# One of three counts per search step moved from VectorE to ScalarE, which sums signs, in the expert routing of a fused transformer kernel

## The reference

```python
def balanced_assignment(scores):          # scores: [8192 tokens, 8 experts]
    T, E = scores.shape
    C = T // E
    taken = jnp.zeros((T,), dtype=bool)
    parts = []
    for e in range(E):
        s = jnp.where(taken, -jnp.inf, scores[:, e])
        _, idx = jax.lax.top_k(s, C)
        parts.append(idx)
        taken = taken.at[idx].set(True)
    return jnp.concatenate(parts)
```

## Time and profile before

| | |
|---|---|
| median of 3 runs | 2756.76 us (2747.97 to 2757.8) |
| the profiled execution | 2750.51 us, its span 2748.7 us |
| share of the span: PE, DVE, ACT, POOL | 75%, 72%, 56%, 44% |
| mean granted TensorE clock | 0.89 of full speed |
| routing, first score to last expert | 1084 to 1347 us |
| of it the 112 search steps with what lies between them | 1132.1 to 1338.9 us |
| scatter of the tokens behind it | 1347.5 to some 1440 us |

### The profile page before, as it was taken

One profiled execution on the slowest core, in us unless ns is written; L12 is line 12 of the kernel. 1 busy time (PEld: TensorE's weight loads), 2 busy tenths in 40 slices (PEclk: granted clock), 3 DMA queues, 4 the chain that ended last, 5 costly groups with the idle time before them and its releaser, 6 DMA issues. The chain is left out here.

```text
span 2748.7 us, 73587 instructions
## 1 busy us (share of the span) xinstructions
PE 2061.8 (75%) x26748; PEld 1195.5 (43%) x26748; DVE 1992.3 (72%) x5289; ACT 1552.3 (56%) x2872; POOL 1218.4 (44%) x1067
## 2 busy tenths in 40 slices
PE   5988989888988896411009928888888888888587
PEld 3776767676767675400004402232222322322354
DVE  4676767676777666688407817898888988987698
ACT  5665656565655563100004416787777777877587
POOL 5666666666667562000263357632432343230122
PEclk9999999999999998555559968999999999999799
DMA  4333333333333331000022232221112212220001
GB/s 115 75 79 72 71 77 74 75 80 72 79 76 75 71 73 25 1 0 0 19 64 76 81 70 49 51 41 27 25 32 34 33 26 31 35 32 2 13 23 35
DMA packets 103680, 136.73 MB, mean 50 GB/s; under 512 B 23781, under 2 KB 78981, under 8 KB 103046
## 3 DMA queue, kind: packets, MB, share of 16 engines
q1 hardware_dynamic: 99206, 123.34, 20.7%
q0 software_dynamic: 4096, 8.40, 1.1%
HBM read 26.52 MB, written 12.58 MB: 14 GB/s over the span
## 5 line engine op out<-in xcount | busy, mean ns | idle before, releaser
L1788 DVE TENSOR_REDUCE d_nmax_<-d_s_ 128x2 bf16<-128x1024 f32 x512 | 614.9, 1222 | 128.6 <-PE d_s_ L1950 126.9
L1699 ACT ACTIVATE d_pT_<-d_t_ 128x512 f32<-128x512 f32 x1024 | 558.2, 601 | 170.8 <-PE d_t_ L1962 163.3
L268 POOL TENSOR_TENSOR a_other<-a_other,a_rope 128x512 f32<-128x512 f32 x256 | 323.2, 1284 | 358.0 <-DMA a_other<-a_raw 357.2
L1975 PE MATMUL d_o_<-d_pT_,d_v_ 128*32 128x256 f32 x4096 | 326.3, 403 | 0.2 <-ACT d_pT_ L1699 0.2
L1962 PE MATMUL d_t_<-d_qs_,d_ks_ 49*128 49x512 bf16 x1024 | 207.7, 402 | 86.8 <-ACT d_pT_ L1699 41.6
L336 ACT ACTIVATE a_pT<-a_t 64x384 f32<-64x384 f32 x512 | 248.3, 485 | 19.2 <-PE a_t L588 7.5
L476 DVE RECIPROCAL a_rden<-a_o 128x512 f32<-128x512 f32 x64 | 214.7, 3355 | 49.5 <-PE a_o L601 49.4
L299 ACT COPY a_v<-a_proj 128x512 f32<-128x512 f32 x128 | 74.9, 585 | 278.8 <-PE a_proj L499 278.8
L460 DVE TENSOR_REDUCE a_nmax<-a_s 128x4 bf16<-128x384 f32 x256 | 130.7, 552 | 134.7 <-PE a_s L565 134.3
L1950 PE MATMUL d_s_<-d_ks_,d_qs_ 48*128 48x512 bf16 x1024 | 206.9, 400 | 17.5 <-DVE d_nmax_ L1788 12.1
L1155 ACT ACTIVATE c_hT_<-c_in_,c_beta_,c_gamma_ 128x512 f32<-128x512 f32 x16 | 12.4, 777 | 328.0 <-PE c_in_ L1275 328.0
(11 more groups left out here) (260 smaller groups left out, 4641.6 us busy)
## 6 DMA issues: line engine op xcount, KB each, us to landing
a_other<-a_raw SPq DMA_DIRECT2D x512, 128.0 KB, 2.3
d_qs_<-d_part_ SPq DMA_DIRECT2D x192, 64.0 KB
d_ks_<-d_part_ SPq DMA_DIRECT2D x192, 64.0 KB
a_xpre<-x SPq DMA_DIRECT2D x16, 256.0 KB, 3.8
a_xres<-x SPq DMA_DIRECT2D x16, 256.0 KB, 3.5
c_xs_<-sorted_x SPq DMA_DIRECT2D x16, 256.0 KB, 2.7
c_w_<-e_w SPq DMA_DIRECT2D x16, 256.0 KB, 3.3
sorted_x<-c_xs_ SPq DMA_DIRECT2D x16, 256.0 KB, 2.0
```

The lines of the kernel that those rows point to most:

```text
L268: nc.gpsimd.tensor_tensor(other[s % 2][:, side, :], other[s % 2][:, side, :], rope[:, 1, :], ALU.mult).then_inc(rope2_done, 1)
L1699: nc.scalar.activation(pT[kt][pair][:, a, :], t_bank(j, turn)[:], ACT.Exp).then_inc(t_read, 1)
L1788: nc.vector.reduce_max(out, s_bank(unit, e)[:], AX_X, negate=True).then_inc(s_read, 1)
L1975: ins = nc.tensor.matmul(o_ps[HC * i:HC * (i + 1), cols], v[e.k][:, kt, g * GH + i, :], pT[kt][i // 2][:, i % 2, cols], start=(kt, half) = ...
```

## The change

In a search step VectorE counts for the first two thresholds only. For the third, ScalarE takes the sign of (threshold - value) over the same 64 values with an accumulator output, in one ACTIVATE. The threshold is shifted by 0.5, so that no value equals it. The sum of signs is 64 - 2 x (count), and so the count is 32 - 0.5 x (sum of signs). TensorE puts this together in column 2 of `tot`: a matmul of ones with `halves` (which holds 32) that is issued ahead of time, and one of a matrix of -0.5 with `signs`. The sums thus come from three matmuls in place of one. `tot` is now two PSUM tiles used in turn. Some constants are set at the start of the routing.

```diff
-        count = sb("count", [128, TIES], BF16)
+        count = sb("count", [128, TIES - 1], BF16)
+        signs = sb("signs", [128, 1], BF16)
+        junk_s = sb("junk_s", [128, TILES])
+        minus_half = sb("minus_half", [128, 128], BF16)
+        halves = sb("halves", [128, 1], BF16)
...
-        tot = ps("tot", [128, 512])
+        tot = [ps(f"tot{k}", [128, 512]) for k in range(2)]
...
+            def signed(values, e, n, link):
+
+                act.wait_ge(chain, PER * e + DONE + link)
+                with nc.allow_low_precision(reason="whole numbers up to 64"):
+                    nc.scalar.activation(junk_s[:], values, ACT.Sign, bias=tries[:, TIES - 1:TIES], scale=-1.0,
+                                         accum_out=signs[:]).then_inc(signs_ready, 1)
+                act.wait_ge(signs_ready, 2 * DIGITS * e + n + 1)
+
+            with act.Fori(0, E - 1) as e:
+                for d in range(DIGITS):
+                    signed(a1[:], e, d, 1 + 3 * d if d else 2)
+                for d in range(DIGITS):
+                    signed(b1[:], e, DIGITS + d, 3 * (DIGITS + 1 + d) if d else 3 * DIGITS + 4)
...
             with pe.Fori(0, E - 1) as e:
                 for n in range(CNT):
-                    pe.wait_ge(cnt_ready, CNT * e + n + 1)
-                    nc.tensor.matmul(tot[:, 0:TIES], ones[:], count[:], start=True, stop=True).then_inc(tot_ready, 1)
+                    tot_n = tot[n % 2]
+                    if n % (DIGITS + 1) < DIGITS:
+                        nc.tensor.matmul(tot_n[:, 2:3], ones[:], halves[:], start=True, stop=True,
+                                         skip_group_check=True)
+                        pe.wait_ge(cnt_ready, CNT * e + n + 1)
+                        nc.tensor.matmul(tot_n[:, 0:2], ones[:], count[:], start=False, stop=True,
+                                         skip_group_check=True)
+                        pe.wait_ge(signs_ready, 2 * DIGITS * e + n - n // (DIGITS + 1) + 1)
+                        nc.tensor.matmul(tot_n[:, 2:3], minus_half[:], signs[:], start=False, stop=True,
+                                         skip_group_check=True).then_inc(tot_ready, 1)
...
+            nc.vector.memset(halves[:], TILES / 2.0)
...
+            nc.vector.memset(minus_half[:], -0.5).then_inc(set_ready, 1)
...
                     for d in reversed(range(DIGITS)):
-                        for k in range(TIES):
+                        for k in range(TIES - 1):
                             ins = nc.vector.tensor_scalar(junk[:, k, :], values, tries[:, k:k + 1], None, ALU.is_ge,
                                                           ALU.add, accum_out=count[:, k:k + 1])
```

More of the change, by code:

```diff
@@ L749, in routing @@
         cnt_ready = sem("cnt_ready")
+        signs_ready = sem("signs_ready")
+        set_ready = sem("set_ready")
         tot_ready = sem("tot_ready")
@@ L757, in routing @@
         CNT = 2 * DIGITS + 2
+        PER = 6 * DIGITS + 14
+        DONE = 5
         GROUPS = TILES // G4
@@ L833, in _ @@
             scores(GROUPS - 1, 1)
+            pe.wait_ge(set_ready, 1)
             def ranks(flags, n):
@@ L842, in _ @@
                 for n in range(CNT):
-                    pe.wait_ge(cnt_ready, CNT * e + n + 1)
-                    nc.tensor.matmul(tot[:, 0:TIES], ones[:], count[:], start=True, stop=True).then_inc(tot_ready, 1)
+                    tot_n = tot[n % 2]
[8 more added lines that the diff above has]
+                                         skip_group_check=True).then_inc(tot_ready, 1)
+                    else:
+                        pe.wait_ge(cnt_ready, CNT * e + n + 1)
+                        nc.tensor.matmul(tot_n[:, 0:2], ones[:], count[:], start=True, stop=True,
+                                         skip_group_check=True).then_inc(tot_ready, 1)
                 ranks(tied, 2 * e + 1)
@@ L864, in _ @@
             nc.vector.memset(count[:], 0.0)
+            nc.vector.memset(halves[:], TILES / 2.0)
             for d in range(DIGITS):
                 for k in range(TIES):
-                    nc.vector.memset(steps[:, d, k:k + 1], float((k + 1) * 4 ** d))
+                    nc.vector.memset(steps[:, d, k:k + 1], (k + 1) * 4.0 ** d - (0.5 if k == TIES - 1 else 0.0))
             for k in range(TIES):
-                nc.vector.memset(first[:, k:k + 1], float((k + 1) * 4 ** (DIGITS - 1) + 1))
+                nc.vector.memset(first[:, k:k + 1],
+                                 (k + 1) * 4.0 ** (DIGITS - 1) + (0.5 if k == TIES - 1 else 1.0))
+            nc.vector.memset(minus_half[:], -0.5).then_inc(set_ready, 1)
             def kept(m, k):
@@ L900, in _ @@
             link(nc.vector.tensor_scalar(lo1[:], half_j[:], 1.0, None, ALU.add))
-            done = chained[0]
+            assert chained[0] == DONE
+            done = DONE
             def expert(e, last):
@@ L917, in total @@
                     ins.then_inc(cnt_ready, 1)
-                    return lambda: dve.wait_ge(tot_ready, CNT * e + totals[0])
+                    tot_n = tot[(totals[0] - 1) % 2]
+                    return tot_n, lambda: dve.wait_ge(tot_ready, CNT * e + totals[0])
                 def search(values, needed, thr):
@@ L961, in expert @@
                     search(a1[:], need[0], thr[0])
-                    total(nc.vector.tensor_scalar(above[:], a1[:], thr[0][:], None, ALU.is_gt, ALU.add,
-                                                  accum_out=count[:, 0:1]))()
+                    tot_n, wait_total = total(nc.vector.tensor_scalar(above[:], a1[:], thr[0][:], None, ALU.is_gt, ALU.add,
+                                                                   accum_out=count[:, 0:1]))
+                    wait_total()
                     nc.vector.tensor_scalar(eq[:], a1[:], thr[0][:], None, ALU.is_equal)
-                    link(nc.vector.tensor_tensor(need[1][:], need[0][:], tot[:, 0:1], ALU.subtract))
+                    link(nc.vector.tensor_tensor(need[1][:], need[0][:], tot_n[:, 0:1], ALU.subtract))
                     link(nc.vector.tensor_tensor(b1[:], eq[:], lo1[:, e, :], ALU.mult))
                     search(b1[:], need[1], thr[1])
-                    total(nc.vector.tensor_scalar(above2[:], b1[:], thr[1][:], None, ALU.is_gt, ALU.add,
-                                                  accum_out=count[:, 0:1]))()
-                    nc.vector.tensor_tensor(need[2][:], need[1][:], tot[:, 0:1], ALU.subtract)
+                    tot_n, wait_total = total(nc.vector.tensor_scalar(above2[:], b1[:], thr[1][:], None, ALU.is_gt, ALU.add,
+                                                                   accum_out=count[:, 0:1]))
+                    wait_total()
+                    nc.vector.tensor_tensor(need[2][:], need[1][:], tot_n[:, 0:1], ALU.subtract)
                     ins = nc.vector.tensor_scalar(tied[:], b1[:], thr[1][:], None, ALU.is_equal)
@@ L984, in expert @@
                 assert last or (step[0] == PER and totals[0] == CNT)
-            PER = 6 * DIGITS + 14
             with dve.Fori(0, E - 1) as e:
```

4 lines of the change are left out of this document (2 added, 2 removed).

## The result

The changed kernel takes 2768.42 us (median of 9 runs, 2760.78 to 2782.81), the kernel before 2750.68 in the runs beside it. The ratio is 1.0067, with a 95% interval from 1.0039 to 1.0095: slower by 0.7%, where 0.45% less was forecast. The profiled execution took 2762.82 us, its span is 2761.0.

A forecast was written before the change was run, and what follows sets the result against it. The searches' single chain without slack, mostly VectorE, was taken as the bound; per step -0.20 + 0.09 = -0.11 us, times 112 = -12.3 us, so 2756.8 becomes 2744.5 us, 0.45% less, range 2734 to 2757.

The forecast's parts named there:

- A count removed: Search step on VectorE: one count fewer takes 0.20 us off the chain, times 112 steps -22.4 us.
- The sign: ScalarE's ACTIVATE with accumulator in each search step: 0.34 to 0.53 us, taken as 0.43, hidden behind VectorE's two counts.
- The late sign: Rival in the search step: ScalarE needs 0.60 to 0.70 us, gain shrinks to 0 to 11 us, 2751 us; chance 0.10.
- the slower rival: Search step: the sign path takes longer than three counts; at 0.86 us it costs 19 us, 2776 us; chance 0.05.
- The second matmul: TensorE's signs matmul behind the counts' matmul in each step: adds 0.09 us, bounds 0.04 and 0.16; times 112 +10.1 us.
- The nearly free second matmul: Rival in the search step: second matmul costs 0.03 us or less, at least 19 us gained, 2738 us; chance 0.07.
- The sum for the searches: All search steps: -0.20 + 0.09 = -0.11 us per step, times 112 = -12.3 us.
- A microsecond off the searches is a microsecond off the span: Searches, 1132.1 to 1338.9 us: nothing else is under way and GpSimd's scatter waits, so savings reach the span fully.
- What costs nothing: Routing: new constants, unchanged last counts and ranks, and longer loops add no time; even a 3.93 us stall would nearly fit.

The follow-up runs named there:

- group 2: Changed kernel with both TensorE waits (signs, then counts) ahead of both matmuls, same number of instructions; ratio to the kernel before 1.0065.
- Groups 1 and 6: Kernel before plus idle TensorE matmuls: 80 instructions 1.0106, 256 0.9993, 96 1.0010; changed kernel plus 176: 0.9994; both waits first, all three engines padded: 0.9926.

## Why the prediction was wrong, point by point

- *A count removed, 0.20 us per step.* Right: the two counts start 0.20 apart, the accumulator is read 0.41 behind the start.
- *The sign, 0.34 to 0.53 us, taken as 0.43.* Right in kind. The ACTIVATE took 0.348 us (0.343 worked out from the earlier trace rows), its accumulator read is an instruction of 0.188 us that starts 0.26 behind it. The end is at 0.45. The late sign and the slower rival, both built on a long sign, did not happen.
- *The second matmul, 0.04 to 0.16, taken as 0.09.* Right: 1.434 - 0.20 + 0.08 = 1.315 us per step (0.09 by the two matmul rows). Its composition was less so: with nothing between the two matmuls (group 2) a step is 0.034 us shorter, so some 0.045 stay for the second matmul, where 0.02 were taken for it and 0.08 for what stands between. The 0.09 of the sum was my estimate between its bounds, and no run shows its parts as they were taken; what the runs showed in its place is 0.08 for the whole: those 0.045, and 0.034 for what stands between. The nearly free second matmul did not happen, and not even group 2 reaches its 0.03.
- *The sum for the searches.* 12.3 us forecast, 13.6 less in the routing measured; 0.119 x 112 = 13.3.
- *"A microsecond off the searches is a microsecond off the span."* As a statement on the chain it held (the scatter starts 13.6 us sooner, relative to the routing's start); what failed is that nothing else would be touched.
- *"What costs nothing"* is the step that failed. I looked at the longer loops inside the routing, where indeed nothing stalls, and had the row of a 3.93 us stall behind a branch in hand, but asked only whether it could arise in the searches. The 80 instructions also move every later loop of TensorE. Groups 1 and 6 show this in the kernel before, without any of the change: 80 are slower by 0.4 to 1.7%, 96 and 256 are not. It was no rival and had no chance in the text. Part of its size was in reach: a stall of 2 to 3 us in each of five turns, 11.4 us in all. The 28.7 us that the main part grew were not.

How it adds up, from the profiled executions: 1.7 us earlier at the routing's start, 13.6 us less in the routing, 2.2 us less in the head of the second attention and 0.2 in the last stage, and against it 28.7 us in its main part and 1.3 in scatter and experts: 12.3 us more in the span (2748.7 to 2761.0).

What stays open. The kernels padded on TensorE alone lost the slowdown, but show between 0.0 and 0.6% of gain where the searches give 0.5 to 0.6%; with all engines' code put back on whole packets it was 0.63 and 0.74% (for ScalarE and VectorE a packet of 256 instructions was my estimate, made after q8; no run shows theirs). That the other engines' code is the rest is suggested by this, and not shown: restoring one of them gave 0.21 and 0.36%, within each other's intervals, and moving ScalarE's alone cost nothing clear. What made the main part 887.0 us in two kernels without the second stall, and what the extra stalls on the fourth chip are, is open too. Profiles are of one execution each, and single runs of a kernel lie 16 to 48 us apart. That the place of TensorE's code is the cause of the slowdown is shown by groups 1 and 6. That TensorE goes on only after a packet of q8 has landed, 1.5 to 2.2 us behind it at the first stall and 1.2 to 1.6 at the second, is shown by the times of the packets. That the packet ends close behind the target is read from these times, the place of the stall, the step from 80 to 96 and the five packets; where in the code a packet ends the profile doesn't tell.

## What to carry to other kernels

Instructions added to TensorE moved all its later code, and a loop that stands there gained a stall of 1.8 to 3.5 us behind each of its five branches back with 80 instructions and had none of these with 96 (shown here on TensorE alone). So a small gain (here 13.6 us) is to be judged stage by stage: first the edited stage, then the unedited ones, by their waits without a releaser. If an unedited stage changed, try the old kernel with as many idle instructions as the edit added, and the new one with a few more: 16 idle instructions took away here the stall that 80 had brought, and a version with all three engines padded was 0.6 to 0.7% faster than before.

Two waits were cheaper ahead of a pair of small matmuls than between them (0.034 us per pair, 3.8 us in the routing), where the second signal comes first anyway.

## What the runs showed of the hardware that I had not expected

- A stall of 1.8 to 3.5 us between two matmuls of one pair, without a wait, in the first instructions of a loop's turn, present with 80 further instructions ahead of the loop (in all four profiles of such kernels), absent with 0, 96, 176 and 256, and with it five more packets in the instruction queue than with 96 or 176. TensorE goes on 1.2 to 1.6 us after a packet of that queue has landed. On the chips where both were profiled, the main part was 11 to 31 us longer with it (890.1 and 901.7 us against 870.9 and 878.9; 899.8 against 873.8, 875.1 and 879.3). The stalls themselves are 11 to 14 us of that.
- A register instruction and a wait between two small matmuls of TensorE put their weight loads 0.08 us apart instead of 0.01 and the matmuls 0.09 instead of 0.04; moved ahead of the pair they cost 0.034 us less per step.
- The accumulator read of ScalarE is an instruction of 188 ns that starts 0.26 us behind the start of a 348 ns ACTIVATE, so the pair takes 0.45 us.
- The kernel before took 2750 to 2756 us on three chips and 2773.7 on a fourth, where the profiles of four versions show 9 to 12 stalls on d_t where the others have 5 or 6. The extra ones lie ahead of the loop's first branch back, and in two of the four profiles one of them is 13 to 14 us long.
